# Cross-attention and mixture FFN on one core: the FFN in PSUM banks of its own between the attention steps, scores one batch ahead, all four searches in one step

## The reference

```python
x = x + xattn(layernorm(x), ctx, ctx, mask, WQ, bQ, WK, bK, WV, bV, Wp, bp)
x = x + ffn(layernorm(x), W1, b1, W2, b2, gamma, beta, Wr, br)
# xattn: softmax(Q K^T * mask) / 4 @ V @ Wp + bp, heads taken from rows of 256 by a plain reshape
# ffn: out = sum_e probs[:, e] * (gelu(x @ W1s[e] + b1s[e]) @ W2s[e] + b2s[e])
#   probs = softmax of the router's 8 logits on a layernorm of x
#   expert 0 has the clean weights; experts 1 to 7 all have the same perturbed ones:
#   w -> w - 0.8 w for the largest 5% by |w|, w -> w + 0.8 w for the smallest 5%
```

## Time and profile before

| | us |
|---|---|
| device time, three runs | 836.33, 839.43, 840.46 |
| profiled execution, device time | 837.27 |
| its span | 835.5 |
| PE busy in the span | 718.3 (86%) |
| DVE busy | 525.4 (63%) |
| ACT busy | 316.0 (38%) |
| POOL busy | 291.2 (35%) |
| mean granted PE clock | 0.898 of 2.4 GHz |

### The profile page before, as it was taken

How to read it: one execution, slowest core, us unless ns; L and a number is a source line. 1 busy time by engine, 2 the same in 40 slices (tenths; PEclk the granted TensorE clock), 3 DMA queues, 4 the chain that set the end, 5 groups by cost and what they waited for, 6 DMA issues and landing times.

```text
span 835.5 us, 15333 instructions
## 1 busy us (share of the span) xinstructions
PE 718.3 (86%) x5346; PEld 605.3 (72%) x5346; DVE 525.4 (63%) x1327; ACT 316.0 (38%) x428; POOL 291.2 (35%) x288
## 2 busy tenths in 40 slices
PE   3438758898898859989989989989896999999996
PEld 2426656787787748878878878888674888888884
DVE  3698468547857976776776776666499334333441
ACT  1302201333442324444444444443352444555442
POOL 2246034225625732762753753735381000000000
PEclk9758757679799959999999999979897999999999
DMA  5851510420341115044044033023020122222121
GB/s 162 192 136 51 112 43 22 96 66 27 101 109 32 51 54 115 27 111 105 26 119 98 25 104 90 26 76 102 26 77 15 61 76 75 75 75 72 41 63 50
DMA packets 128571, 62.36 MB, mean 75 GB/s; under 512 B 101520, under 2 KB 118800, under 8 KB 128528
## 3 DMA queue, kind: packets, MB, share of 16 engines
q1 hardware_dynamic: 128528, 61.81, 28.0%
HBM read 34.51 MB, written 23.09 MB: 69 GB/s over the span
## 4 chain that ended last, share of the span: by engine, by line
PE 66%; DVE 21%; issue 6%; POOL 4%; ACT 1%; DMA 0%; DVEq 0%; ACTq 0%; POOLq 0%
PE ps_y L337 8%; PE ps_y L338 8%; PE ps_y L339 8%; PE ps_l L337 7%; PE ps_l L338 7%; PE ps_l L339 7%; PE ps_m L591 6%; DVE ind L1212 5%; POOL xh L993 3%; PE ps_m L678 3%; PE ps_s L337 2%; PE ps_s L339 2%; PE ps_s L338 2%; DVE region_a L1113 2%; PE ps_m L626 2%
## 5 line engine op out<-in xcount | busy, mean ns | idle before, releaser
L874 ACT ACTIVATE region_b<-ps_l,bias 128x512 f32<-128x512 f32 x128 | 88.1, 689 | 196.7 <-PE ps_l L339 193.7
L1025 POOL TENSOR_TENSOR region_c_lo<-region_b,region_c_hi 128x512 fp32r<-128x512 f32 x64 | 98.0, 1547 | 142.9 <-ACT region_c_hi L877 142.9
L1212 DVE TENSOR_SCALAR ind<-key,cand 128x2048 bf16<-128x2048 uint16 x124 | 116.1, 978 | 5.0 <-PE ps_m L678 3.0
L1442 DVE TENSOR_TENSOR region_c_lo<-region_b,region_c_hi 128x512 fp32r<-128x512 f32 x64 | 44.1, 692 | 109.0 <-ACT region_c_hi L877 104.6
L337 PE MATMUL ps_l<-x2s_hi,w_hi 128*128 128x512 f32 x256 | 108.0, 422 | 5.0 <-DVE x2s_lo L1076 5.0
L678 PE MATMUL ps_m<-ones_bf,ind 128*128 128x1 bf16 x1984 | 63.2, 164 | 51.6 <-DVE ind L1212 48.2
L337 PE MATMUL ps_y<-region_c_hi,w_hi 128*128 128x512 f32 x256 | 103.9, 406 | 1.6 <-POOL region_c_lo L1025 1.6
L678 PEld LDWEIGHTS ps_m<-ones_bf,ind 128*128 128x128 bf16 x1984 | 58.4, 99 | 62.7 <-DVE ind L1212 56.4
L338 PE MATMUL ps_l<-x2s_lo,w_hi 128*128 128x512 f32 x256 | 103.5, 404 | 0.0
L339 PE MATMUL ps_l<-x2s_hi,w_lo 128*128 128x512 f32 x256 | 103.4, 404 | 0.0
L339 PE MATMUL ps_y<-region_c_hi,w_lo 128*128 128x512 f32 x256 | 101.6, 397 | 0.0
(11 more groups left out here) (173 smaller groups left out, 1232.8 us busy)
## 6 DMA issues: line engine op xcount, KB each, us to landing
acc_scr<-acc SPq DMA_DIRECT2D x8, 514.0 KB, 4.8
acc<-acc_scr SPq DMA_DIRECT2D x8, 514.0 KB, 3.3
xa<-in_x SPq DMA_DIRECT2D x8, 512.0 KB, 5.2
q_scr<-qn_hi SPq DMA_DIRECT2D x16, 256.0 KB, 4.5
q_scr<-qn_lo SPq DMA_DIRECT2D x16, 256.0 KB, 4.6
qs_hi<-q_scr SPq DMA_DIRECT2D x8, 512.0 KB, 4.1
qs_lo<-q_scr SPq DMA_DIRECT2D x8, 512.0 KB, 5.0
x<-in_x SPq DMA_DIRECT2D x32, 128.0 KB, 3.6
```

The source lines that it names most:

```text
L874: act.activation(g[:, f % 4, :], ps_l[:, f % 2, :], ACT.Gelu_apprx_tanh, bias=bias[:, e, f:f + 1]).then_inc(s["gelu"].handle, 1)
L1025: pool.tensor_tensor(gs[1][:, f % 4, :], g[:, f % 4, :], gs[0][:, f % 4, :].bitcast(F32), ALU.subtract).then_inc(s["g_lo"].handle, 1)
L1212: dve.tensor_scalar(ind[s % 2][:], key[:, key_of[rnd][s], :], cand[:, s:s + 1], None, ALU.is_le).then_inc(ind_ready.handle, 1)
L1442: dve.tensor_tensor(gs[1][:, f % 4, :], g[:, f % 4, :], gs[0][:, f % 4, :].bitcast(F32), ALU.subtract).then_inc(s["g_lo"].handle, 1)
```

## The change

The FFN keeps ps_l and ps_y to itself, and all attention work goes through ps_s (the router, the values and the counts stay in ps_m). The pieces h(0) to h(7) and o(0) to o(7) of the FFN of batch i - 1 are spread over the whole body of batch i, where before h(0) came after the third values. All four scores of batch i + 1 are made and masked in body i; the probabilities get four buffers. The outputs have the activations as stationary operand and W2 as moving operand, 256 columns wide, so y comes out by token: `turn_y` and `bias_y` go, and the bias is added by a new DVE function, `base`, ahead of `mix`. A search step compares with all four candidates at once in four buffers; bodies 0 to 6 have four steps each and body 7 none. The start loads and splits in another order, and the keys of batch 0 go from SBUF to their block-diagonal place without DRAM (`load_first_keys`). The small perturbations and `base` stand ahead of the splits in `last_expert`, and the b2 row is now perturbed as 128x256.

```diff
         def turn_queries_input(b):
             wait(pe, ln[0]["xhat"], b)
-            wait(pe, ex[0]["mixed"], b - 3)
+            if not isinstance(b, int) or b > 0:
+                wait(pe, pT_ready, b - 1, 1)
...
-        def turn_probs(b, j):
+        def turn_probs(b, j, last=False):
+
             wait(pe, p_exp, b, j + 1)
             if j == 0:
-                wait(pe, ex[0]["g_hi"], b - 2)
-            elif j < NT - 1:
+                wait(pe, s_masked, b)
+            elif j == 1 and not last:
+                wait(pe, xT_lo, b + 1)
+            elif j == 2 and not last:
+                wait(pe, q_lo, b + 1)
+            else:
                 wait(pe, pT_ready, b, j)
...
-            for m in range(DC):
-                mm = three(pe, ps_y[:, m, :], [w[:, f * D + m * P:f * D + (m + 1) * P] for w in w2s],
-                           [t[:, f % 4, :] for t in gs], f == 0, f == FC - 1)
+            for t in range(NT):
+
+                mm = three(pe, ps_y[:, t // 2, (t % 2) * D:(t % 2) * D + D], [a[:, f % 4, t * P:(t + 1) * P] for a in gs],
+                           [w[:, f * D:(f + 1) * D] for w in w2s], f == 0 and t % 2 == 0, f == FC - 1 and t % 2 == 1)
             mm.then_inc(s["y_step"].handle, 1)
...
+            turn_probs(i, 0, last)
             h(0)
+            values(i, 0)
+            if not last:
+                turn_queries_input(i + 1)
+            h(1)
+            c(0)
+            turn_probs(i, 1, last)
+            h(2)
+            values(i, 1)
+            t(0)
+            if not last:
+                queries(i + 1)
+            o(0)
+            h(3)
+            turn_probs(i, 2, last)
+            o(1)
+            values(i, 2)
+            turn_probs(i, 3, last)
+            c(1)
+            h(4)
             values(i, 3)
+            t(1)
+            o(2)
+            h(5)
             turn_output(i)
+            o(3)
+            c(2)
             project(i)
+            t(2)
+            h(6)
+            o(4)
+            if not last:
+                scores(i + 1, 0)
+            h(7)
+            if not last:
+                scores(i + 1, 1)
+            o(5)
             turn_x2(i)
+            o(6)
+            if not last:
+                scores(i + 1, 2)
             router(i)
+            c(3)
             o(7)
             if not last:
+                scores(i + 1, 3)
+            t(3)
...
-        def mix(e, b, src):
+        def base(e, b):
 
             s = ex[e]
-            wait(dve, s["y_turned"], b)
...
             for t in range(NT):
                 weight = p0[:, t:t + 1] if e == 0 else acc[:, t, D:D + 1]
-                base = keep[:, t, :] if e == 0 else acc[:, t, 0:D]
-                dve.scalar_tensor_tensor(acc[:, t, 0:D], src[:, t // 2, (t % 2) * D:(t % 2) * D + D], weight, base,
+                onto = keep[:, t, :] if e == 0 else acc[:, t, 0:D]
+                dve.scalar_tensor_tensor(onto, b2row[:, e, :], weight, onto, ALU.mult, ALU.add).then_inc(s["based"].handle, 1)
```

More of the change, by code:

```diff
@@ L616, in turn_x2 @@
             wait(pe, x2_ready, b)
+            if not isinstance(b, int) or b + 1 < B:
+                wait(pe, s_masked, b + 1, 2 * DC)
             for c in range(DC):
@@ L694, in keys_values @@
                 mm.then_inc(kv_product, 1)
-        def step(k):
-            count(k, 0)
-            count(k, 1)
-            total(k)
         pe.wait_ge(ld_ctx, 16)
@@ L878, in gelu @@
                            bias=bias[:, e, f:f + 1]).then_inc(s["g_hi"].handle, 1)
-        def bias_y(e, b):
-            s = ex[e]
-            wait(act, s["y_step"], b)
-            wait(act, s["y_turned"], b - 1)
-            for m in range(DC):
-                act.activation(yT[:, m, :], ps_y[:, m, :], ACT.Identity,
-                               bias=bias[:, e, FC + m:FC + m + 1]).then_inc(s["y_biased"].handle, 1)
         def high_x2(b):
@@ L1059, in body @@
                 normalise(0, i + 2, xa)
+            for f in range(3, FC - 2):
+                low(f)
+            rsqrt(1, i)
+            normalise(1, i, x2)
+            low(6)
+            if not last:
+                shift(i + 1, 0)
+            low(7)
+            if not last:
+                shift(i + 1, 1)
+            router_rsqrt(i)
             if not last:
@@ L1390, in body @@
                 mask_scores(i + 1, 2)
+            logits(i)
+            if not last:
+                counts(k + 3)
             if not first:
-                mix(0, i - 1, ps_y)
+                mix(0, i - 1)
+            if not last:
+                mask_scores(i + 1, 3)
+                decide(k + 3)
         steps = [0]
@@ L1423, in last_expert @@
             split_x2(0)
[L1424 to L1425 removed]
             wait(dve, ex[0]["y_step"], B - 1)
             split([t[:] for t in w2s], wagain[:, 1, :], pw_hi, 2, pw_lo)
[L1428 to L1429 removed]
+            mix(0, B - 1)
         pipeline(dve, body, second_round, last_expert)
@@ L1436, in perturbed_expert @@
                 split_x2(b)
+                mix(1, b - 1)
             for f in range(FC):
-                if f == 2 and not first:
-                    mix(1, b - 1, ps_m)
                 wait(dve, s["g_hi"], b, f + 1)
```

523 lines of the change are left out of this document (251 added, 272 removed).

## The result

The changed kernel took 853.1 us (median of four runs, 849.26 to 863.02) against 837.88 for the kernel before on the same chip: a ratio of 1.0163, 95% interval 1.0112 to 1.0215. The prediction was 819, with a range of 800 to 845.

| stage | before | predicted | after |
|---|---|---|---|
| start | 72.6 | 71 | 92.4 |
| body 0 | 64.7 | 66 | 69.1 |
| body 1 | 78.1 | 67 | 66.3 |
| body 2 | 68.2 | 65 | 65.6 |
| body 3 | 74.5 | 79 | 79.0 |

A forecast was written before the change was run, and what follows sets the result against it. PE was taken as the bound in bodies 4 to 6 and expert 1. Stages from start (71) through bodies of about 65 to expert 1 (183) and end summed to 816.5, written down as 819 us, range 800 to 845.

The forecast's parts named there:

- Start: the K path is shortened: Before body 0: direct keys and scores between steps, against an earlier fourth score and mask; 71 us, 1.6 less.
- the start's growth past 76: Stretch before body 0: a start longer than 76 us was named as a sign that the prediction is wrong.
- The spacing of 0.12 us for 256 columns: Output matmuls: twelve of 256 columns take 1.44 us; starts over 0.125 us apart would show it wrong.
- Eight batches at 22.7: Expert 1: each batch takes 22.7 us (8 x 1.40 + 8 x 1.44), with 1.5 for the cold start 183.
- 57.9 and 1 more for the clock: New body: PE's own work 57.9 us; a clock drop after a wait costs 1 to 2 us more.
- (a): End of the body: PE waits about 4 us for the last mask, which stands behind mix on DVE.
- (b): Start of the body: PE's transposes wait 1.2 us for xT_lo, behind ACT's exponential, table load and gelu.
- (c): Around project: PE waits 1 us for oT_lo, as comparison 2 lies ahead of it on DVE.
- "No effect": Rival: waits only move, bodies take 61.5 + 1.8, only body 7's steps are saved; 830 us; chance 0.15 shared with DVE leading.
- "The clock stays low": Rival: PE runs at 1.2 GHz from the body's end until the queries; bodies of 70, 849 us; chance 0.15.
- set waits but not the pace: Rival that DVE leads: POOL stretches comparisons to 1.2 us, bodies of 68, 837 us; chance 0.15 shared with effects cancelling.
- bodies did not reach 61: Rival that the gaps close: the end wait shrinks to 1.9 us, project's vanishes; bodies of 61, 795 us; chance 0.15.

The follow-up runs named there:

- `mask_first`: Changed kernel with batch 0's mask load issued ahead of the first keys' loads on SP's queue; 849.2 us, ratio 1.0126.
- `mask_steps`: Changed kernel with the mask load ahead of the first keys' loads and the search steps ahead of batch 0's scores and masks; 837.4 us, ratio 0.9949.
- `dram_steps`: Changed kernel with the first keys through DRAM again and three search steps ahead of batch 0's scores and masks; 836.4 us, ratio 0.9973.
- `x2_exp1`: Changed kernel with short start, x2 transposes behind all four scores, and expert 1's last output among the next batch's hidden pieces; 817.4 us, ratio 0.9742.
- `before_steps`: Kernel before with only the steps moved: four in each of bodies 3 to 6, none in body 7; 865.5 us, ratio 1.0304.
- `act_keys`: `mask_steps` with the eight loads of the first keys' high part moved from SP's to ACT's queue; 836.1 us, ratio 0.9949.

## Why the prediction was wrong

**The step that failed: "Start: the K path is shortened ... 71 (-1.6; 66 to 75)".** It was one sentence without a walk. The direct path has fewer hops than the one through DRAM, but it costs twice the issues on SP, the mask and the values stand behind them in the new order of that queue, and DVE's first mask operation was put ahead of the steps that had filled this time. The start was 92.4. Putting the mask ahead gave back 9.4 of it and the steps ahead 9.9; together they make 73.1, 0.5 above the kernel before. That is shown by `mask_first` and `mask_steps`. I had named the start's growth past 76 as a sign of being wrong, and gave it no rival and no share of the range. Without these 21.4 us the time would have been 831.7, inside the range; `dram_steps`, with the old start, measured 836.4.

**Expert 1, mis-sized by 4.0 us.** The spacing of 0.12 us for 256 columns was right. Eight batches at 22.7 were not: each takes 23.17. The eight transposes of `turn_y` that were removed had stood between the second and the third hidden piece, and had hidden a hand-over: the third piece waits for the first gelu of the batch. `x2_exp1` puts an output in that place and gets 183.1.

**Body 0, 3.1 us over.** Its clock is 0.60 where it was 0.68, and PE is busy for 55 us instead of 48 with as many matmuls (461 against 460), so it is the clock and not more work. Why it is lower there was not tried.

**What held, in part by luck.** Bodies 4 to 6 took 65.9 each where 65 was forecast. PE was busy for 61.0 where I had 57.9 and 1 more for the clock, which falls two or three times in a body and not once; and it waited 4.8 us where I had 6.2: (a) 4.3 instead of 4, (b) nothing instead of 1.2, (c) 0.5 instead of 1. The two errors nearly cancel. That (b) vanished because the work ahead of it ran at half clock is likely, but not shown. Body 1 fell by 11.8 (forecast 11), body 3 was 79.0, body 7 with the gap 83.1 against 84. Here too the reason was partly wrong: "No effect" took a fourth step to cost 1.8 us in the old order, and `before_steps` shows 7 to 18 a body in its longest execution, most of it by the clock (0.78 in bodies 4 and 6).

**The rivals.** None of them was it: the mean clock stayed at 0.92 in the bodies (not 0.56 until the queries), so "The clock stays low" was right that it falls each time and wrong on how long, DVE at 51.5 us of 65.9 set waits but not the pace, and bodies did not reach 61.

## What to carry to other kernels

Walk the start and each DMA queue with the same care as the steady state: count every issue that is put in front of another load, and ask which in-order engine stands first for the load that is now last. When an operation is removed, look for what it was hiding; and where an engine waits at a body's end, move only what nobody behind it needs.

## What the runs showed of the hardware

A DMA of this small kind (8 KB, `load_first_keys`) takes SP 0.59 to 0.70 us to issue. Beside POOL's operations a comparison of 0.35 us took 3.99, until POOL's row had ended, and four full-size ones took 5.9 us instead of 2.74. After waits of 0.7 us (ahead of `project`) to 5.3 us in sum (2.8 and 2.5 ahead of body 5) PE ran at its lower clock, and at the end of five bodies of six it did so behind 16 matmuls of 8 columns and 64 of one column, with no wait. How long it stayed there varied from 3 us to a stretch of 27 us at 0.55 to 0.60, with PE busy nearly throughout (12 us at 0.50 in body 5 of `act_keys`, where PE was busy for 11.99):

```profile
419.40:431.40 12.00, 11.99 (x46) 10.51 (x46) 8.50 (x17) 5.77 (x7) 3.17 (x2) 0.50 0.46 150
```

Extra matmuls in place of the wait for the counts did not change that. Why one body recovers at once and the next does not is open.
